# A four-layer network on one core: the stages between layers get four buffers and scale on ScalarE, the expert stage routes before its table is written and computes its shared expert later

## What is computed

```python
xn = _layernorm(x)                      # (x - mean) / sqrt(var + 1e-5) over 128 channels
s = mixer(xn)
g = _silu(ffn(xn))
x = x + s * g

# _L2_ffn_ref: 64 experts, 8 per token, at most 64 tokens per expert
scores = sigmoid(tokens @ router_w)
# best 4 of 8 groups by their best score, then the best 8 experts of those groups
topk_w = 2.5 * topk_w / sum(topk_w)
pos = how many earlier choices fell on the same expert;  valid = pos < 64
dispatch[e, pos] = tokens[t]
expert_out = (silu(dispatch @ gate_w) * (dispatch @ up_w)) @ down_w
output[t] += expert_out[e, pos] * topk_w * valid
sg = silu(tokens @ shared_gate_w) * (tokens @ shared_up_w)
output = output + sg @ shared_down_w
```

## Time and profile before

| | us |
|---|---|
| median of the runs | 9283.21 |
| the profiled execution | 9277.52 |
| its span, first to last instruction | 9275.7 |
| n0, n1, n2, n3, n4 | 42.10, 53.62, 52.43, 52.56, 32.59 |
| expert stage of layer 2 | 342.93 |
| all other stages together | about 8700 |

### The profile page before, as it was taken

The page is one execution under the profiler, slowest core; times in us unless marked ns, Lnnn a source line. Parts: engine busy times, 40 slices in busy tenths (PEclk is TensorE's granted clock), DMA queues, the critical chain, the costliest instruction groups (busy, mean ns, idle before and its releaser), DMA issues. The chain is left out here.

```text
span 9275.7 us, 216671 instructions
## 1 busy us (share of the span) xinstructions
PE 7053.4 (76%) x72180; PEld 4817.1 (52%) x72628; DVE 6068.0 (65%) x12819; ACT 5394.3 (58%) x13666; POOL 4177.2 (45%) x3667
## 2 busy tenths in 40 slices
PE   5767888888888888888888849997888747633357
PEld 2325665665565566565555638886555512222245
DVE  6876776766767677676667736666666668744432
ACT  4446777777777777777777724444666644311112
POOL 4555554555555555555555514444444445521000
PEclk8889999999999999999999969998999978866578
DMA  2320000000000000000000010000000033222000
GB/s 115 122 88 15 10 10 22 12 11 19 13 11 17 15 11 10 22 10 11 20 12 11 17 64 5 5 5 15 16 19 16 14 131 121 106 74 70 19 0 27
DMA packets 166840, 305.70 MB, mean 33 GB/s; under 512 B 23432, under 2 KB 123168, under 8 KB 147744
## 3 DMA queue, kind: packets, MB, share of 16 engines
q1 hardware_dynamic: 140752, 262.32, 8.7%
q10 hardware_dynamic: 18768, 23.20, 0.7%
q0 software_dynamic: 6144, 5.25, 0.4%
HBM read 208.74 MB, written 31.64 MB: 26 GB/s over the span
## 5 line engine op out<-in xcount | busy, mean ns | idle before, releaser
L822 ACT ACTIVATE L0f_scores<-L0f_scores,L0f_nmx,L0f_rn 128x128 f32<-128x128 f32 x3072 | 1339.1, 443 | 86.4 <-DVE L0f_nmx L926 85.3
L1008 PE MATMUL L0f_ring<-L0f_wqkv,L0f_hT 128*128 128x512 f32 x2324 | 1224.0, 633 | 104.9 <-DMA L0f_scales<-L_ffn_scales_dram 59.9
L752 POOL TENSOR_TENSOR L0f_qr<-L0f_qs,L0f_table 128x512 f32<-128x512 f32 x776 | 989.5, 1275 | 547.0 <-ACT L0f_qs L793 480.8
L759 POOL TENSOR_TENSOR L0f_qr<-L0f_qr,L0f_m 128x512 f32<-128x512 f32 x776 | 986.0, 1271 | 278.1 <-issue 131.8
L766 POOL TENSOR_TENSOR L0f_qr<-L0f_qr,L0f_rn 128x512 f32<-128x512 f32 x388 | 396.2, 1042 | 786.5 <-DVE L0f_rn L918 784.9
L924 DVE TENSOR_REDUCE L0f_mx<-L0f_scores 128x8 f32<-128x1024 f32 x384 | 469.4, 1222 | 360.8 <-PE L0f_scores L1036 183.9
L895 DVE TENSOR_TENSOR L0f_m<-L0f_ring,L0f_table 128x512 f32<-128x512 f32 x776 | 522.1, 688 | 262.5 <-ACT L0f_qs L793 241.7
L822 ACT ACTIVATION_READ_ACCUMULATOR L0f_scores<-L0f_scores,L0f_nmx,L0f_rn 128x1 f32 x3072 | 668.5, 218 | 0.0
L837 ACT ACTIVATE L0f_oT<-L0f_o 128x512 f32<-128x512 f32 x385 | 235.4, 611 | 639.5 <-PE L0f_o L1074 597.5
L1008 PEld LDWEIGHTS L0f_ring<-L0f_wqkv,L0f_hT 128*128 128x128 f32 x2324 | 396.9, 197 | 382.1 <-issue 289.9
L1070 PE MATMUL L0f_o<-L0f_pT,L0f_vb 128*64 128x96 f32 (+1 forms) x6160 | 501.7, 280 | 97.3 <-DVE L0f_pT L941 81.5
(11 more groups left out here) (533 smaller groups left out, 19082.7 us busy)
## 6 DMA issues: line engine op xcount, KB each, us to landing
L0a_bc_all<-L0a_bc_rows SPq DMA_DIRECT2D x32, 2048.0 KB, 11.3
L2a_bc_all<-L2a_bc_rows SPq DMA_DIRECT2D x32, 2048.0 KB, 11.3
L0f_vmix<-L0f_vb SPq DMA_DIRECT2D x288, 128.0 KB, 2.3
L1f_vmix<-L1f_vb SPq DMA_DIRECT2D x96, 128.0 KB, 2.3
L0f_wqkv<-L_ffn_wqkv_dram SPq DMA_DIRECT2D x7, 1536.0 KB, 6.0
L2f_parts<-L2f_zero ACTq DMA_DIRECT2D x10, 832.0 KB, 13.8
n_s<-mixer_out SPq DMA_DIRECT2D x32, 256.0 KB, 4.1
L2f_back<-L2f_parts SPq DMA_DIRECT2D x32, 256.0 KB, 4.0
```

The costliest lines, as they stand in the source:

```text
L752: e.tensor_tensor(rotated, qs[:, q % QN], spread(cos, 1, 8), ALU.mult).then_inc(cosed.sem, 1)
L759: e.tensor_tensor(rotated, rotated, m2[:, q % SN], ALU.add).then_inc(added.sem, 1)
L822: a = e.activation(s_ps[:, h, j], s_ps[:, h, j], ACT.Exp, bias=nmx[:, s, col:col + 1], scale=rn[:, tt, 2 * u, col:col + 1], accum_out=sums ...
L1008: e.matmul(bank[:], hT[:, tt * P:tt * P + P], wqkv[:, col:col + 512], start=True, stop=True).then_inc(full, 1)
```

## The change

**Stages between layers** (n0 to n4): loops over pairs become straight code over 8 batches. xb, s and xo have four buffers, statistics and roots two. GpSimd also makes `shifted = -mean / sqrt(var + eps)`, and ScalarE scales the four tiles (Identity with scale and bias) instead of VectorE. Silu runs up to two batches ahead. The stores go from ScalarE's queue to SyncE's, behind all loads. VectorE's sum of batch b waits for the store and the scaling of batch b - 4.

**Expert stage**: TensorE's first wait counts only router and the three shared expert matrices (`small_in`). The write of the tokens to the table is cut into eight and counts on `table_in`, for which only the gathers wait. The zero fills (now eight of 1088 KB) and the weight loads are issued by ScalarE after the sigmoid of the third batch. The shared expert leaves the routing and runs one batch per set of experts (`share`), in banks 2 and 3 of `big`; the experts' down projection keeps banks 0 and 1 alone. Table and `parts` hold token t of a batch in row 4 * (t % 128) + t // 128, so that what a partition reads or writes there is one piece of 4 rows where the rows are whole; VectorE turns the row numbers accordingly with six more small operations.

```diff
@@ moe_net
-    ROWS = TOKENS + CAP
+    ROWS = TOKENS + TT * CAP
-    WIDE = 13 * C
+    WIDE = 17 * C
-        back = r.sb("back", [P, NR, TT, COPIES, C])
+        back = r.sb("back", [P, NR, COPIES, TT, C])
         @block.sync
-            for dst, src in ((router, "router"), (sg, "sg"), (su, "su"), (sd, "sd"), (slot, "slot")):
-                e.dma_start(dst[:], w[src]).then_inc(loaded, 16)
+            for dst, src in ((router, "router"), (sg, "sg"), (su, "su"), (sd, "sd")):
+                e.dma_start(dst[:], w[src]).then_inc(small_in, 16)
+            e.dma_start(slot[:], w["slot"]).then_inc(loaded, 16)
-            e.dma_start(table[0:TOKENS, 0:C].rearrange("(t p) c -> p t c", p=P), g.f[:]).then_inc(loaded, 16)
+            for b in range(BATCH):
+                e.dma_start(table[b * SEQ:b * SEQ + SEQ, 0:C].rearrange("(p t) c -> p t c", t=TT),
+                            g.f[:, b * TT:b * TT + TT]).then_inc(table_in, 16)
...
-                    e.dma_start(back[:, b % NR, :, c], rows.rearrange("(t p) c -> p t c", p=P)).then_inc(back_in[b % NR], 16)
+                    e.dma_start(back[:, b % NR, c], rows.rearrange("(p t) c -> p t c", t=TT)).then_inc(back_in[b % NR], 16)
         @block.gpsimd
-            e.wait_ge(loaded, SMALL)
-            e.wait_ge(table_in, 16 * (BATCH + 1))
+            e.wait_ge(table_in, TABLE)
         @block.scalar
-            for i in range(ZEROS // 13):
-                e.dma_start(wide[:, i * WIDE:i * WIDE + WIDE], zero[:]).then_inc(parts_zero, 16)
-            for dst, src in ((wg, "wg"), (wu, "wu"), (wd, "wd")):
-                e.dma_start(dst[:], w[src]).then_inc(weights_in, 16)
...
                 e.activation(score[:, b % 2], l_ps[:, 0:TT * E].rearrange("p (t c) -> p t c", t=TT),
                              ACT.Sigmoid).then_inc(scored, 1)
-                if b >= 2:
-                    silu(b - 2)
+                if b == 2:
+                    for i in range(ZEROS // 17):
+                        e.dma_start(wide[:, i * WIDE:i * WIDE + WIDE], zero[:]).then_inc(parts_zero, 16)
+                    for dst, src in ((wg, "wg"), (wu, "wu"), (wd, "wd")):
+                        e.dma_start(dst[:], w[src]).then_inc(weights_in, 16)
...
                 e.activation(sil2[:, s % 2], g_ps[:, 0:PER * CAP], ACT.Silu).then_inc(gated, 1)
+                share(s)
         @block.vector
-                e.wait_ge(silued, b + 1)
-                e.wait_ge(su_full, b + 1)
-                e.tensor_tensor(shared[:, b], u_ps[0:I], sil[:, b % 2], ALU.mult).then_inc(shared_ready, 1)
...
             e.tensor_scalar(row[:], row[:], float(TOKENS), None, ALU.add)
+            e.drain()
+            for i, size in enumerate((SEQ, P)):
+                e.tensor_scalar(lower[i][:], row[:], 0.5 - size / 2, size * ROUND, ALU.add, ALU.add)
+            e.drain()
+            for i, size in enumerate((SEQ, P)):
+                e.scalar_tensor_tensor(within[i][:], lower[i][:], size * ROUND, row[:], ALU.subtract, ALU.subtract)
+            e.drain()
+            e.scalar_tensor_tensor(row[:], within[0][:], 1.0 - 1.0 / P, row[:], ALU.mult, ALU.add)
+            e.drain()
+            e.scalar_tensor_tensor(row[:], within[1][:], 1.0 / P - TT, row[:], ALU.mult, ALU.add)
...
             for s in range(SETS):
                 gate(s)
                 if s:
                     weigh(s - 1)
+                share(s)
         @block.tensor
-            e.wait_ge(loaded, SMALL)
+            e.wait_ge(small_in, SMALL)
...
             for b in range(BATCH):
                 route(b)
-                if b >= 2:
-                    share(b - 2)
-            for b in range(BATCH - 2, BATCH):
-                share(b)
+                if b:
+                    turn_choice(b - 1)
+            turn_choice(BATCH - 1)
...
             def down(s):
                 e.wait_ge(h_ready, s + 1)
-                if s >= 2:
-                    e.wait_ge(y_ready, s - 1)
+                if s:
+                    e.wait_ge(y_ready, s)
...
                 project(s)
                 if s:
                     down(s - 1)
+                share(s)
@@ combine
+        NBUF = 4
         @block.sync
+            for b in range(BATCH):
+                k = b % NBUF
+                if b >= NBUF:
+                    e.wait_ge(added, b - NBUF + 1)
                 e.dma_start(xb[:, k], view(x_in, b)).then_inc(loaded[k], 16)
                 if mixed:
                     e.dma_start(sb_[:, k], view(g.s_dram, b)).then_inc(loaded[k], 16)
+            if x_out is not None:
+                for b in range(BATCH):
+                    e.wait_ge(added, b + 1)
+                    e.dma_start(view(x_out, b), xo[:, b % NBUF]).then_inc(sent[b % NBUF], 16)
         @block.scalar
-                    e.wait_ge(*added(h, k, 2))
-                    e.activation(fb[:, k], g.f[:, bass.ds(b * TT, TT), :], ACT.Silu).then_inc(silued.sem, 1)
-                if x_out is not None:
-                    e.wait_ge(*added(h, k))
-                    e.dma_start(view(x_out, b), xo[:, k]).then_inc(sent[k], 16)
+            def silu(b):
+                if b >= 2:
+                    e.wait_ge(added, b - 1)
+                e.activation(fb[:, b % 2], g.f[:, b * TT:b * TT + TT, :], ACT.Silu).then_inc(silued, 1)
+            def norm(b):
+                e.wait_ge(rstd_ready, b + 1)
+                for tt in range(TT):
+                    o = e.activation(g.f[:, b * TT + tt, :], xo[:, b % NBUF, tt], ACT.Identity,
+                                     bias=shifted[:, b % 2, tt:tt + 1], scale=rstd[:, b % 2, tt:tt + 1])
+                o.then_inc(normed, 1)
+            if mixed:
+                for b in range(2):
+                    silu(b)
+            for b in range(BATCH):
+                if mixed and b + 2 < BATCH:
+                    silu(b + 2)
+                if again:
+                    norm(b)
         @block.gpsimd
+                    e.tensor_tensor(shifted[:, k], rstd[:, k], mv[:, k, :, 0], ALU.mult)
+                    e.drain()
+                    e.tensor_scalar(shifted[:, k], shifted[:, k], -1.0, None, ALU.mult)
+                    e.drain().then_inc(rstd_ready, 1)
         @block.vector
+                if b >= NBUF:
+                    if x_out is not None:
+                        e.wait_ge(sent[k], 16 * (b // NBUF))
+                    if again:
+                        e.wait_ge(normed, b - NBUF + 1)
+                if mixed:
+                    e.tensor_tensor(xo[:, k], sb_[:, k], xb[:, k], ALU.add).then_inc(added, 1)
...
-                e.wait_ge(*rstd_ready(h, k))
-                for tt in range(TT):
-                    e.tensor_scalar(g.f[:, bass.ds(b * TT + tt, 1), :].rearrange("p o c -> p (o c)"), xo[:, k, tt],
-                                    mv[:, tt, 0:1], rstd[:, tt:tt + 1], ALU.subtract, ALU.mult)
```

More of the change, by code:

```diff
@@ L2443, in _ @@
                 for c in range(COPIES):
-                    e.matmul(bank, g.ident[:], back[:, b % NR, :, c, :], start=c == 0, stop=False)
+                    e.matmul(bank, g.ident[:], back[:, b % NR, c], start=c == 0, stop=False)
                 for tt in range(TT):
@@ L3108, in body @@
[L3108 to L3113 removed]
+                    e.bn_aggr(mv[:, b % 2, tt], stats[:, b % 2, tt])
+                e.drain().then_inc(measured, 1)
 class Shared:
```

145 lines of the change are left out of this document (68 added, 77 removed).

## The result

The changed kernel takes 9060.17 us (median of 4 runs, 9059.18 to 9080.25) against 9283.09 us before: a ratio of 0.9768, 95% interval 0.9751 to 0.9785. The profiled execution's span fell from 9275.7 to 9057.6 us. One execution each of e18 and e19, further down, took 27268 and 22241 us at a granted clock of 0.55 and 0.44; it counts in their medians and not in their ratios.

The account below looks back on a forecast made before the run. One core runs stages in series with barriers, so stage savings add up: minus 71.3 us between layers and minus 71.7 in the expert stage make minus 143.0, giving a median of 9140 us, range 9117 to 9168.

Parts of the forecast that it names:

- n4: Last stage between layers: becomes bound by transfers, 28.5 us against 32.59, minus 4.1 (0 to 7).
- Start: Expert stage: TensorE waits for four small loads only, first transpose 3.4 us after the stage begins, minus 45.4.
- picking: Expert stage, VectorE picking tokens, 47.50 us before: six more row-number operations add 1.5 us (1 to 2.5).
- ScalarE's eleven issues: Expert stage: zero fills and weight loads take about 11 us of ScalarE's queue; VectorE stands still 8 us (0 to 12).
- the routing: Expert stage: shared expert's wait leaves VectorE's chain, 62.0 us against 80.30, minus 18.3.
- Reading back: End of expert stage: 2 KB pieces instead of 512 bytes speed the loads, minus 9.5 us (0 to 11).
- three times 1.4, twice 1.7, and 1.5: Read-back saving: three waits lose 1.4 us each, two also the slow clock's 1.7, the first wait 1.5.
- rival 1: Expert stage's read-back gains nothing, since latency and issue set landing, not piece size: 9150 us; chance 0.14.
- Rival 4: Better than forecast: ScalarE issues faster and stores land before they are wanted, minus 14, 9126 us; chance 0.07.
- rival 6: Expert stage: scatters slow down with the new row numbers, 7 us each giving 9297 us; chance 0.02.

Follow-up runs that it names:

- e18: Changed kernel plus ten empty drains on VectorE in each of the 48 passes of the first layer's local attention: 9140.39 us, ratio 0.9849.
- e19: Kernel before plus ten empty drains on GpSimd in each of the 48 passes of the first layer's local attention: 9250.98 us, ratio 0.9977.
- e8: Changed kernel with table and copy rows back in the old order, so read-back moves 512 B pieces: 9073.75 us, ratio 0.9774.

## Why the prediction was wrong

**The step that failed** is the first: "a change inside a stage shortens the whole by what that stage loses, and the rest need not be modelled". The new code of n0 is 51 instructions longer on VectorE, and that moved the loop of L0f, which runs 48 times, out of a place that cost it 70.2 us. Without these the forecast for the profiled execution was 9134.5 us against 9057.6 + 70.2 + 1.8 = 9129.6 (1.8 as before, around the span).

That the touched parts came to 140.3 us against 143.0 is in part luck: stages between layers 75.5 for 71.3, expert stage 64.8 for 71.7, with the misses on opposite sides.

**Stage between layers.** Right in each part to within 2.1 us. n0 26.22 (26.1 forecast), n1 to n3 35.55, 34.66 and 34.90 (35.8). VectorE is busy 21.09 us in them (21 said), and stops once, before the fifth sum, for a store: 2.35 us (2 said). n4 was taken 2.1 us too long: it ran at 238 GB/s, where I had used 193 of the earlier trace rows.

**Expert stage.** Start 3.61 us (3.4 said), picking 49.11 (49.0), gathers 40.42 (40.3), scatters 66.37 (67.9). ScalarE's eleven issues took 12.7 us instead of 11, VectorE stood 9.5 instead of 8, and the routing took 64.0 instead of 62.0. **Reading back** is the term that was mis-sized: 3.5 us for 9.5. Its own parts (three times 1.4, twice 1.7, and 1.5) add up to 9.1, not 9.5. My 382 GB/s for large pieces came from a stretch in which two queues filled the engines; here eight loads of one queue follow each other. That the rate of one queue is the limit is a guess; no run tried a second one. The rule of the Trainium skill ("DMA: Bandwidth & Descriptors", Specifications) that 512 bytes reach line rate would give 0; e8 shows 4.8, so neither was right, and rival 1 (9150) stood as near as the forecast.

**The rivals.** None of them could have given 9060: each was about a changed stage. Rival 4 had the sign and named the wrong place. Scatters with the new rows (rival 6) took 2.07 us each, no more than before.

## What to carry to other kernels

A long loop of several engines can lie a few tenths of a microsecond beside a collision in each pass, and code put anywhere ahead of it may move it in or out. So read the big untouched loop before and after every change, by its length and by the mean length of its small operations; where it changed, shift it with empty instructions and see if the time follows, before crediting the edit. Where VectorE and GpSimd both work, a short VectorE operation that others wait for belongs where GpSimd isn't in a long one.

## What had not been expected of the hardware

- A small VectorE operation (128x8, 0.17 us) lasted until the GpSimd operation that it met ended: 1.21, 1.20 and 0.71 us in three kernels. All L926 over 0.3 us, 138 to 191 in each of the 20 traces, ended 0.02 to 0.03 us behind such an operation.
- A loop of about 308 instructions on VectorE and one of 304 on ScalarE fetched 5 packets of 8 KB again in most passes or none, by their place. For VectorE 0, 110 and 128 instructions on did, 25, 51, 90 and 179 did not. Which rule sets these borders stays untested.
- The refetching by itself cost nothing that shows (446 packets at 4640.5 us, 266 at 4635.8); the one idle time of 0.39 us that stood ahead of a certain instruction did.
- Ten drains in a loop took 0.41 us on VectorE and 0.87 on GpSimd.
